# One core of Trainium2: the first activations loaded in two transfers, and two context loads issued by ScalarE

## What is computed

```python
def quant(t):                       # one scale for 128 elements of x, for 128x128 of the context
    safe = max(abs(t)) in the block
    return float8(t * 448 / safe) * safe / 448

x = x + tanh(g_xattn) * einsum('emk,enk->emn', quant(layernorm(x)), quant(ctx))
h = layernorm(x)
probs = softmax(h @ gate_w.T); keep the 4 largest of 8 experts, renormalised
moe = sum over experts of comb[:, e] * (silu(h @ wg[e].T) * (h @ wu[e].T)) @ wd[e].T
sh = silu(h @ swg.T) * (h @ swu.T) @ swd.T
out = x + tanh(g_ffn) * (moe + sigmoid(h @ shared_gate_w.T) * sh)
```

## Time and profile before

| What | Value |
|---|---|
| Time, median of 3 runs (lowest to highest) | 182.54 us (182.36 to 183.12) |
| Time of the profiled execution | 183.21 us |
| Its span, from the first to the last instruction | 181.2 us |
| What lies around the span | 2.0 us |
| Granted TensorE clock over the span | 0.999 |
| PE, DVE, ACT, POOL busy | 158.0, 128.8, 102.9, 93.9 us |

### The profile page before, as it was taken

The page is one execution under the profiler, slowest core; times in us unless marked ns, Lnnn a source line. Parts: engine busy times, 40 slices in busy tenths (PEclk is TensorE's granted clock), DMA queues, the critical chain, the costliest instruction groups (busy, mean ns, idle before and its releaser), DMA issues.

```text
span 181.2 us, 2313 instructions
## 1 busy us (share of the span) xinstructions
PE 158.0 (87%) x723; PEld 122.9 (68%) x723; DVE 128.8 (71%) x265; ACT 102.9 (57%) x229; POOL 93.9 (52%) x92
## 2 busy tenths in 40 slices
PE   0022789999989999999997999999999999999992
PEld 0010358877768777777885887888788888888871
DVE  1898975897997799998766953978368544444463
ACT  2399664949553995583737664444655644443430
POOL 3120715644641578568217995446565655553550
PEclk9999999999999999999999999999999999999999
DMA  5998993000039940000000000200089700000003
GB/s 139 285 399 291 345 326 133 2 0 0 0 60 275 249 114 4 2 2 0 4 0 0 2 0 0 96 24 0 13 218 271 201 0 2 0 0 0 0 0 116
DMA packets 8047, 16.17 MB, mean 89 GB/s; under 512 B 1234, under 2 KB 1234, under 8 KB 8036
## 3 DMA queue, kind: packets, MB, share of 16 engines
q1 hardware_dynamic: 8036, 16.04, 29.8%
HBM read 14.95 MB, written 1.09 MB: 89 GB/s over the span
## 4 chain that ended last, share of the span: by engine, by line
PE 59%; DVE 18%; ACT 13%; issue 5%; DMA 2%; POOL 0%; DVEq 0%
PE bank L968 51%; ACT xc L380 3%; DVE a_lo L750 2%; DVE act L734 2%; ACT cw L372 2%; DMA x<-xs 2%; ACT silu L456 2%; DVE act L744 2%; DVE x L657 2%; PE bank L920 2%; ACT xc L409 2%; PE bank L1010 1%; DVE bn L568 1%; ACT gu_hi L442 1%; DVE amax_x L612 1%
## 5 line engine op out<-in xcount | busy, mean ns | idle before, releaser
L315 POOL TENSOR_TENSOR gu_lo<-w_raw,gu_hi 128x512 fp32r<-128x512 f32 (+1 forms) x34 | 47.5, 1396 | 22.9 <-ACT gu_hi L442 15.2
L322 POOL TENSOR_TENSOR d_lo<-w_raw,d_hi 128x256 fp32r<-128x256 f32 x34 | 33.9, 998 | 39.6 <-ACT d_hi L447 39.5
L968 PE MATMUL bank<-h_hi,gu_hi 128*128 128x512 f32 x124 | 49.4, 398 | 0.6 <-ACT silu L456 0.4
L968 PE MATMUL bank<-h_hi,gu_lo 128*128 128x512 f32 x124 | 49.2, 397 | 0.0
L968 PE MATMUL bank<-h_lo,gu_hi 128*128 128x512 f32 x124 | 49.1, 396 | 0.0
L456 ACT ACTIVATE silu<-bank 128x512 f32<-128x512 f32 (+1 forms) x34 | 20.2, 595 | 43.5 <-PE bank L968 42.5
L744 DVE TENSOR_TENSOR act<-silu,mixw 128x512 f32<-128x512 f32 x18 | 14.6, 812 | 21.4 <-ACT silu L456 21.4
L750 DVE TENSOR_TENSOR a_lo<-act,a_hi 128x512 fp32r<-128x512 f32 x32 | 28.1, 877 | 1.1 <-ACT a_hi L464 1.0
L968 PEld LDWEIGHTS bank<-h_hi,gu_hi 128*128 128x128 f32 x124 | 23.3, 188 | 6.5 <-issue 1.2
L968 PEld LDWEIGHTS bank<-h_hi,gu_lo 128*128 128x128 f32 x124 | 23.3, 188 | 5.5
L968 PEld LDWEIGHTS bank<-h_lo,gu_hi 128*128 128x128 f32 x124 | 23.4, 189 | 5.3
(11 more groups left out here) (117 smaller groups left out, 191.8 us busy)
## 6 DMA issues: line engine op xcount, KB each, us to landing
w_raw<-w_full SPq DMA_DIRECT2D x16, 384.0 KB, 4.7
mixw<-comb_d SPq DMA_DIRECT2D x10, 256.0 KB, 5.5
x<-xs SPq DMA_DIRECT2D x4, 256.0 KB, 6.8
cw<-ctx_t SPq DMA_DIRECT2D x4, 256.0 KB, 6.0
out_t<-fin SPq DMA_DIRECT2D x4, 256.0 KB, 2.3
mixw<-comb_d SPq DMA_DIRECT2D x4, 224.0 KB, 5.3
mixw<-comb_d SPq DMA_DIRECT2D x4, 192.0 KB, 5.1
mixw<-comb_d SPq DMA_DIRECT2D x4, 160.0 KB, 4.6
```

What stands on the lines that cost most here:

```text
L315: nc.gpsimd.tensor_tensor(gu_lo[:, slot, 0:cols], w_raw[:, c, 0:cols], gu_hi[:, slot, 0:cols].bitcast(F32), ALU.subtract).then_inc(gu_lo_d ...
L322: nc.gpsimd.tensor_tensor(d_lo[:, slot, :], w_raw[:, c, at:at + D], d_hi[:, slot, :].bitcast(F32), ALU.subtract).then_inc(d_lo_done, 1)
L968: last = nc.tensor.matmul(out, w[k][a], x_of[k][b], start=(start and k == 0 and i == 0), stop=(stop and k == blocks - 1 and i == 2))
```

## The change

`x` of batch 0 comes in two transfers, one for each tile: 128 KB each, 1 KB for each partition, each with a semaphore of its own. `bn_stats` of a tile waits for the semaphore of that tile. The contexts of batches 0 and 1 are not issued by SyncE behind `x` any more: ScalarE issues them as its first two instructions, ahead of the load of its table. `load_w(0)` and all behind it on SyncE come one transfer earlier in its list.

```diff
+        x0_landed = [sem(f"x0_landed{j}") for j in range(BT)]
         x_landed = [sem(f"x_landed{b}") for b in range(B)]
...
+            def load_first_x():
+                for j in tiles(0):
+                    sp.dma_start(x[:, j, :], xs[:, j, :]).then_inc(x0_landed[j], 16)
...
-            load_x(0)
-            load_ctx(0)
-            load_ctx(1)
+            load_first_x()
             load_w(0)
             load_x(1)
...
         @block.scalar
         def _(a):
+            for b in range(HB):
+                a.dma_start(cw[:, b], ctx_t[:, b]).then_inc(ctx_landed[b], 16)
             a.preload_act_table(ACT.Silu)
...
             def moments(which, b):
                 for j in tiles(b):
+                    if which == 0 and b == 0:
+                        v.wait_ge(x0_landed[j], 16)
                     last = nc.vector.bn_stats(bn[:, which, j, :], x[:, j, :])
...
             def stats_x(b):
-                v.wait_ge(x_landed[b], 16)
+                if b > 0:
+                    v.wait_ge(x_landed[b], 16)
                 stats(0, b, moments(0, b)).then_inc(var_ready, 1)
```

## The result

The time rose from a median of 182.83 us (182.36 to 183.81, 6 runs) to 185.42 us (184.4 to 186.35, 6 runs). The ratio is 1.0123, with a 95% interval of 1.0087 to 1.0158, so the loss is 1.6 to 2.9 us, about 2.25; the two medians differ by 2.59. The profiled execution has a span of 184.2 us, 3.0 more than before. It took 186.35 us, the longest of the six, so the 3.0 of the two profiles is somewhat more than the loss of the runs. The forecast was 183.2 us with a range of 182.1 to 184.5; the measured time lies above it.

A forecast was written before the change was run, and what follows sets the result against it. The prediction took the start to be bound by the procession of first loads, with no slack behind `x`. The second `bn_stats` ending +0.65 later gave 183.86, less 0.67 for the profiled execution's excess over the median: 183.2 us, range 182.1 to 184.5.

The forecast's parts named there:

- I take this middle one: First loads: two queues share by equal bytes or whole transfers; second tile lands at 5.0, +0.65 us; chance 0.44.
- packet by packet: First loads: engines alternate single rows between queues, `x` gets a third of the bytes; +2.2 to +2.4 us; chance 0.17.
- The gain of the split: VectorE's `bn_stats` pair: the first runs while tile 1 is under way, gaining 0.37 us if landing is unchanged.
- the later issue of the second tile: SyncE's start: the second tile is asked for 0.45 us later, costing 0 to 0.45; taken as 0.
- The price of the middle case: First loads: 524 KB ahead of the second tile's end make it land at 5.0, costing +0.65 us.
- the byte's turn plus 1.0 us: Landings of the first loads: one queue serves in order, and landing follows the byte's turn by some 1.0 us.
- The start has no slack: Chain from `x` of batch 0: each link starts about 0.02 us after the last, so lateness passes on us for us.
- ScalarE's issues and the later table load: ScalarE's start: two issues delay the table load to end between 2.9 and 3.5, before `centre(0)` at 5.33; cost nothing.
- `max_ctx(1)` had no wait: Sign on VectorE in the profile after: the maximum of ctx(1) would not wait for its transfer.
- The rival of a late ctx(1): First loads: weights sharing with ctx(1) make it hold up the scales of `x`; 183.2 to 183.8 us; chance 0.10.

The follow-up runs named there:

- run 4: The full change, but each context comes in two transfers with rows of 1 KB, still from ScalarE: ratio 1.012 to the kernel before.
- run 2: The kernel before with only the contexts of batches 0 and 1 moved to ScalarE, `x` in one transfer: ratio 1.0051 to the kernel before.
- run 9: The full change, but ScalarE issues both contexts as one transfer with rows of 4 KB: ratio 1.0089 to the kernel before.
- run 5: The full change, but ScalarE issues only ctx(0); SyncE issues ctx(1) behind the two tiles: ratio 0.9987 to the kernel before.
- run 6: The kernel before on SyncE alone, but with both contexts issued ahead of `x`, in whole transfers: ratio 1.0161 to the kernel before.
- run 7: The full change, but ScalarE issues the second tile of `x`, and SyncE the contexts behind the first tile: ratio 0.9996 to the kernel before.
- run 1: The full change, but both contexts go back to SyncE behind the two tiles, leaving the split alone: ratio 1.0009 to the kernel before.
- run 3: The full change, but ScalarE issues the contexts behind its table load: ratio 1.0118 to the kernel before.
- run 8: The full change with contexts in rows of 1 KB, and SyncE waiting for ctx(1) to land before `load_w(0)`: ratio 1.0052 to the kernel before.
- run 10: The full change, but ScalarE loads its table and waits for the first tile to land before issuing the contexts: ratio 1.0234 to the kernel before.

## Why the prediction was wrong

**The step that failed** is the choice inside the bounds: "I take this middle one". It put 524 KB ahead of the end of the second tile, its landing at 5.0 and the loss at +0.65. The tile landed at 7.0, and the end of its `bn_stats` moved by 2.71. The engines do not take turns by equal bytes or by whole transfers. They take about one packet from each queue in turn, and a packet is one partition's row. Four kernels with the contexts in the same place and different rows show it: for 2 KB of context against 1 KB of `x` 146 to 166 packets in the same stretch; for 4 KB, 59 to 74, with the first tile late by another 1.9 us; for 1 KB against 1 KB (run 4) and 2 KB against 2 KB (run 2) the last of `x` at 4.70 and 4.71 instead of 7.0. Turns of whole transfers would have left `x` at 3.97 in run 2, where it is asked for with the first context and its first row moves first (1.74 against 2.15), and likewise the first tile in its place in run 9 (1.75 against 1.99). The turns are not exact: from 2.0 to 3.5 us run 2 has 62 packets of the contexts to 90 of SyncE's queue, and run 4 has 149 to 202.

This was the rival "packet by packet", which had 0.17 and gave +2.2 to +2.4 us. The measured 2.25 agrees with its price partly by luck, since the second `bn_stats` and `mul_x` are 2.71 late and the median of 185.42 lies above its 184.7 to 185.0. The prediction read a packet as a row from the mean of 2.0 KB. That mean shows no such thing, as it mixes rows of up to 3 KB with 1234 packets under 512 B in the page of before; the stretches above do. DMA: Bandwidth & Descriptors, "Queues, rings and completion order", in the Trainium skill says that an engine goes round its queues packet by packet; the runs agree, with one row to a packet and not the larger number of descriptors that the page calls typical.

**Where the last microseconds go.** The rival had the second tile land at 6.5 to 6.8; it landed at 7.0. Most of its rows were long through. A transfer has landed when all sixteen DMA engines have done their parts of it, and the parts of the second tile landed between 4.06 and 7.00, nine of them by 5.03. What the engines moved from 4.5 to 6.7 us (after) shows the rest:

```profile
DMA packets 275, 0.57 MB, mean 261 GB/s; under 512 B 32, under 2 KB 53, under 8 KB 275
```

The difference of 53 and 32 is the rows of 1 KB: 21 of the 256 of `x` were still to come, the last at 6.58. So the landing is set by the engines that were furthest behind. In run 5 the parts of the same tile landed between 3.64 and 4.36. Why the engines drift apart so much more with both contexts on the second queue was not settled.

The lateness arrives whole at TensorE's first transposes of `h`, which start at 26.76 instead of 24.06, 2.70 later, but the span grew by 3.0. A further term lies at these transposes (L920 before, L928 after): four of them took 1.12 us in the profile after and 0.66 before. TensorE's timeline, of after and then of run 6:

```profile
26.76 1.12 PE L928 MATMUL bank<-eye,xc 128*128 128x128 f32 x4 [0.16 <-ACT xc L414]
```

```profile
27.45 0.66 PE L920 MATMUL bank<-eye,xc 128*128 128x128 f32 x4 [0.22 <-ACT xc L409]
```

Runs 2, 5, 7 and 9 have 1.11 or 1.12 too, runs 1, 3, 4, 6, 8 and 10 have 0.66, and neither lateness nor the kernel sorts them: run 3 repeats the full change and has 0.66. From the start of `mul_x` to the end of the span it is 173.4 to 173.5 us after and in runs 2, 5 and 9, but 173.0 to 173.1 before and in runs 1, 3, 4, 6 and 10 (run 7, whose profile is the longest of its twelve runs, has 174.4). So it adds 0.3 to 0.5 to some profiles and not to others; what makes it so is open.

**The gain of the split** was right in form. The cover is 0.32 and not 0.37, since a `bn_stats` by itself takes 0.43. Its counterpart was mis-sized. For the later issue of the second tile I took 0 within 0 to 0.45; run 1 shows 0.40, so the split gives nothing even without a second queue.

**The price of the middle case** was off too. With 524 KB ahead of the second tile (run 5) it lands near 4.4, not 5.0, and the loss is nil instead of 0.65. Runs 2 and 4, with as many bytes ahead of the last of `x`, have it at 4.7. The rule "the byte's turn plus 1.0 us" is rough: the lag was 0.4 in run 5, 1.0 to 1.3 in the kernel before, and about 1.5 in the full change, and run 6 missed by 0.6 on one queue. It counts the bytes of all sixteen engines together, and the landing goes by the last of them.

**What held.** The start has no slack: in the full change `mul_x` and the end of the second `bn_stats` move by the same 2.71, and in run 6 3.39 at `mul_x` is 3.3 in the span. In the times of the runs a few tenths less arrive: 2.25 for 2.71, 0.9 for 1.14 (run 2), 3.0 for 3.39 (run 6), 1.6 for 2.45 (run 9), 4.3 for 4.81 (run 10). Part of this may be that the lateness is counted from one profile of before, a rather short one (span 181.2, against medians of 181.3 to 181.9 in the groups of runs of before beside the experiments); it was not settled. ScalarE's issues and the later table load cost nothing. `max_ctx(1)` had no wait in the full change. The rival of a late ctx(1) was real all the same: it is the wait in run 2 (0.33) and in run 4 (2.24), and run 8 ties it to the weights.

No version beat the kernel before. Runs 1, 5 and 7 are level with it.

## What to carry to other kernels

One queue in order of need is a priority list; a second queue that is asked at the same time gets about every second turn, whatever is in it. Before a load is moved to another engine's queue, ask which transfer of the first queue has its user waiting, and compare the length of the rows on both sides: the shorter rows lose. Look at the last of the sixteen parts of a transfer and not at the mean, because the user waits for all of them. When loads arrive just ahead of their users, a piece brought forward is paid for by the next in line, so cost each landing against its user and not the first alone; and a transfer cut in two to overlap its halves must gain more than the later issue of the second costs (0.40 us here, against 0.32 gained).

## What the runs showed of the hardware that was not expected

- The load of an activation table does not hold up ScalarE's issue of a transfer behind it: the issue started at 0.76 with the table load running from 0.73 to 2.01 (run 3). The other way round the table load waits for the issues (1.66).
- A transfer issued on the second queue late, behind a filled first queue, can get no turns for a while: in run 10 it was issued at 3.10 and moved nothing until 5.59, while SyncE's queue moved 0.66 MB from 3.1 to 5.4. What decides when a queue gets its first turn was not tested.
- One context beside the two tiles of `x` was carried at no cost to the landing of the second tile: 238 GB/s against 188 from 1.75 to 4.00 (runs 5 and 1). The first tile came 0.75 later.
- The sixteen parts of one transfer of 128 KB can land 2.9 us apart (the second tile in the full change), or 0.7 apart (the same tile in run 5).
